# A six-layer transformer on one core: the products, copies and vector steps of a round placed by quarters

## The chip, the cores and the metric

One NeuronCore of a Trainium2 chip runs the whole program in one launch. The metric is device time in microseconds (us), lower is better. The engines are TensorE (PE; its weight loads PEld), VectorE (DVE), ScalarE (ACT), GpSimd (POOL) and SyncE (SP, which issues the DMAs here). Each takes its own list of instructions in a fixed order, and a wait at one of them holds all that stands behind it in that list.

## What is computed

Two adaptive-layer-norm blocks. Block 0 has a test-time-trained layer and then a six-layer local-attention transformer over 4 sequences of 512 tokens, width 128; block 1 has relative attention and a routed expert layer. The change touches the transformer alone:

```python
for i in range(DEPTH):                                   # 6; B 4, n 512, HEADS 16, DIM_HEAD 64
    x = attn_layer(shift_tokens(x), Wqkv[i], q_scale[i], k_scale[i], Wo[i]) + x
    x = ffn_layer(shift_tokens(x), ln_g[i], ln_b[i], W1[i], b1[i], W2[i], b2[i]) + x

def attn_layer(x, Wqkv, qs, ksc, Wo):
    q, k, v = split_heads(x @ Wqkv)
    q, k = l2norm(q) * qs, l2norm(k) * ksc
    q = q * cos * scale + rotate_half(q) * sin * scale   # rotary tables; k with 1 / scale
    k = k * cos * inv + rotate_half(k) * sin * inv
    return merge_heads(local_attention(q, k, v)) @ Wo    # windows of 32, each sees itself and the one before

def ffn_layer(x, g, bln, W1, b1, W2, b2):
    a, gate = split((layernorm(x) * g + bln) @ W1 + b1)
    return a * gelu(gate) @ W2 + b2
```

## The kernel before

**Units, parts, rounds.** A unit is one sequence in one layer: 24 units. Three kinds of work run side by side for different units. (1) Projections of a unit, in 8 pieces (4 of K, 4 of Q); each piece has two halves, one PSUM bank each. (2) Attention of the unit in 8 parts: 4 tiles of 128 tokens, each in two parts, even and odd, by head. (3) The feed-forward of an earlier unit. `rounds()` counts time in steps; a unit starts every `UNIT` steps, a piece and a part every fourth step, a tile of values every eighth. Four steps are called a round here. In each step every engine writes down what its tables `PART_AT`, `NORM_AT`, `SPREAD_AT`, `SCALE_AT`, `FFN_AT` and the lags place there: parts first, then units, the oldest first. That alone sets the order on each engine; the semaphore waits are written beside each instruction and follow the data.

**A piece.** PE: half 0 and half 1, each three fp32r products of weights and input split into high and low (`three_products`, L1111 to L1113). ACT: a square of each half (L1293, `sq`). DVE: four rotary steps out of the two banks (L1421, `kT`, `qT`, `rotated`). POOL: the sum of the two squares (L1556), then two steps that finish the rotation (L1562, L1563). After every second piece PE sums the squares over rows (L1142, 8 products per piece, fp32), DVE takes them into `norms` (L1431), and after each kind come the roots (L217 to L226). K's roots go through DRAM and come back wide (SP, L957), and scale K (DVE, L1444). Q's are turned (PE, L1146) and copied (ACT, L1298).

**A part.** PE: mask and scores (L1203, L1211). DVE: `keep` (L1486), row maxima (L1491). ACT: eight exponentials with sums (L1357). DVE: reciprocal (L1494). POOL: scaling of p (L1577). PE: turn (L1219, four transposes). ACT: copy of p (L1363). PE: weigh (L1229), p times values. ACT: copy of o (L1368). After an odd part PE mixes with Wo (L1237) and DVE adds to z (L1498).

**Values.** For each tile two value products (L1111 to L1113 with `wqkv` as the moving side), each copied by ACT (L1306), then ten window DMAs (SP, L972 to L977).

**Feed-forward.** PE: center, sum, spread (L1162, L1167, L1173), three gate products (L1180), three up products (L1183), down (L1188); the third of each has 85 rows. ACT: gate copies (L1341), gelu (L1345). DVE: `act` times up (L1464), the last addition (L1468).

**PSUM.** Scores have banks 0 and 1, turn 2, weigh 2 and 3, the halves 4 and 5. Sums, value products, mixes, the turned roots and all feed-forward products share banks 6 and 7 in turn (`ring_take`): a product there waits until the last user but one has been read.

Of the kernel before, what the change touches and what calls it, by code (L numbers as in the profile page):

```python
# [11 lines left out]
ALU = mybir.AluOpType  # L12
# [5 lines left out]
B, S = 4, 512  # L18
# [679 lines left out]
def test_time_pool(c, t, later):  # L698
# [4 lines left out]
    for x in range(DOUBLINGS + 1):  # L703
# [5 lines left out]
UNITS_TF, UNIT, TILE, PART = DEPTH * B, 32, 8, 4  # L709
PARTS = 2 * TPB  # L710
GROUPS_TF, HALF_D = 4, DH // 2
PART_FIRST = 39
PART_AT = {"score": 0, "keep": 0, "largest": 1, "exp": 2, "inverse": 3, "scale": 3, "turn": 5, "turn_copy": 6, "weigh": 6, "o_copy": 8, "mix": 9, "add": 9}
PART_STEPS = 10
VALUE_FIRST, WINDOWS_AT = 29, 31
SHIFT_AT = -4
SQUARES_LAG, SUM_LAG, MADE_LAG = 2, 4, 3
NORM_AT = {"root0": 17, "out": 15, "root1": 33, "turn": 39, "copy": 39}
SPREAD_AT = (16, 18, 19, 24)
SCALE_AT = (24, 28, 29, 32)  # L720
HALF_AT = (0, 1)
FFN_AT = {"shift": 80, "center": 83, "square": 84, "sum": 84, "root": 84, "spread": 88, "scale": 89, "gate0": 91, "gate1": 95, "gate2": 96, "gelu": 99,
          "up0": 100, "up1": 101, "up2": 104, "down": 108, "add": 109}
NORM_SPREAD, NORM_SCALE = 2, {1: 9, 2: 17, 3: 25}
NORM_ENDS = (0, B - 1)
TABLES = (2, 3, 0, 1)
UNIT_STEPS = 110
SPLIT_AT = {2: 13, 3: 31, 0: 39, 1: 40, 4: 56, 5: 59}
# [3 lines left out]
def rounds():  # L732

    for r in range(UNIT * (UNITS_TF - 1) + UNIT_STEPS):
        now = [("spread", b, 0) for b in NORM_SCALE if r == NORM_SPREAD] + [("scale", b, 0) for b, at in NORM_SCALE.items() if r == at]
        for m in range(UNITS_TF * PARTS):
            s = r - UNIT * (m // PARTS) - PART_FIRST - PART * (m % PARTS)
            if 0 <= s < PART_STEPS:
                now.append(("part", m, s))
        for u in range(UNITS_TF):  # L740
            s = r - UNIT * u
            if SHIFT_AT <= s < UNIT_STEPS:
                now.append(("unit", u, s))
        yield now
# [98 lines left out]
def ring_takes(kind, n, s):  # L843

    if kind == "part":
        return ["mix"] * (s == PART_AT["mix"] and n % 2)
    users = []
    if kind == "norm":
        return users
    if SUM_LAG <= s < SUM_LAG + UNIT and (s - SUM_LAG) % 8 == 4:  # L850
        users.append(f"sum{(s - SUM_LAG) // 4}")
    if s == NORM_AT["turn"]:
        users.append("rn")
    if 0 <= s - VALUE_FIRST < UNIT and (s - VALUE_FIRST) % TILE in (0, 2):
        i, f = divmod(s - VALUE_FIRST, TILE)
        users.append(f"v{i}{f // 2}")
    users += [name for name in ("center", "sum", "spread", "gate0", "gate1", "gate2", "up0", "up1", "up2", "down") if FFN_AT[name] == s]
    return users
# [59 lines left out]
def transformer_sync(c, t):  # L918
    SP = c.SP
    for now in rounds():  # L920
        for kind, u, s in now:
# [3 lines left out]
            if b == B - 1 and l + 1 < DEPTH:  # L925
                if s == PART_FIRST + PART * (PARTS - 1) + PART_STEPS - 1:
                    SP.wait_ge(*t.mixed.on((u + 1) * TPB - 1))
                    load_mix(c, t, l + 1)
                if s == FFN_AT["add"]:
                    SP.wait_ge(*t.f_down.on(u))  # L930
                    load_ffn(c, t, l + 1)
                for x, k in enumerate(order()):
                    then, after = (l + 1, x + RAW) if x + RAW < len(SPLIT_AT) else (l + 2, x + RAW - len(SPLIT_AT))
                    if s == SPLIT_AT[k] + 1 and then < DEPTH:
# [185 lines left out]
def unit_tensor(c, t, u, s):  # L1120
    PE, psum, (l, b) = c.PE, c.psum, divmod(u, B)
    xs = [x[:, :] for x in t.xs[u % 2]]
    for at in range(2):
        if not (0 <= s < UNIT and s % 4 == HALF_AT[at]):
            continue
        p = s // 4
# [8 lines left out]
    if SUM_LAG <= s < SUM_LAG + UNIT and (s - SUM_LAG) % 8 == 4:  # L1135
        p = (s - SUM_LAG) // 4
# [11 lines left out]
    if 0 <= i < TPB and at in (0, 2):  # L1148
        f = at // 2
# [132 lines left out]
def unit_scalar(c, t, u, s):  # L1282
# [4 lines left out]
    for half in range(2):  # L1287
        p, at = divmod(s - 1 - HALF_AT[half], 4)
# [10 lines left out]
    i, at = divmod(s - VALUE_FIRST - 1, TILE)  # L1299
    if 0 <= i < TPB and at in (0, 2):  # L1300
        n, f = u * TPB + i, at // 2
# [19 lines left out]
def feed_scalar(c, t, u, s):  # L1321
# [14 lines left out]
    for j, (lo, n) in enumerate(CHUNKS):  # L1336
        if s == FFN_AT[f"gate{j}"] + 1:
# [65 lines left out]

def unit_vector(c, t, u, s):
    V, own, psum, (l, b) = c.V, c.v_own, c.psum, divmod(u, B)
    p, at = divmod(s - 2, 4)
    if 0 <= p < 2 * GROUPS_TF and at == 0:
        kind, g, lo = piece(p)
        cos, sin = (t.tab[:, 2 * (1 - kind) + x, :] for x in range(2))
        first, second = (t.scales[:, kind, half, l:l + 1] for half in range(2))  # L1410
        V.wait_ge(*t.squared.on((u, (p, 0))))
        if u or p:
            V.wait_ge(*t.made.on((u, p - 1) if p else (u - 1, 2 * GROUPS_TF - 1)))
        if u >= 2:
            V.wait_ge(*t.scored.on((u - 1) * PARTS - 1))
        first_half, second_half = made_of(t, u, kind, g)
        rot = [first_half, t.turned_by[0][:, :], second_half, t.turned_by[1][:, :]]
        for half, scale, outs in ((0, first, ((0, cos), (3, sin))), (1, second, ((1, sin), (2, cos)))):
            V.wait_ge(*t.squared.on((u, (p, half))))
            for x, table in outs:  # L1420
                last = V.e.scalar_tensor_tensor(out=rot[x], in0=psum[:, 4 + half, :], scalar=scale, in1=table, op0=ALU.mult, op1=ALU.mult)  # L1421
            last.then_inc(*t.rotated.by((u, (p, half))))
    p, at = divmod(s - SUM_LAG - 1, 4)
# [24 lines left out]
def feed_vector(c, t, u, s):  # L1448
# [11 lines left out]
    for j, (lo, n) in enumerate(CHUNKS):  # L1460
        if s == FFN_AT[f"up{j}"] + 1:
# [84 lines left out]
def unit_gpsimd(c, t, u, s):  # L1546
# [3 lines left out]
    p, at = divmod(s - SQUARES_LAG, 4)  # L1550
# [6 lines left out]
    p, at = divmod(s - MADE_LAG, 4)  # L1557
# [938 lines left out]
```

## Time and profile before

| | |
|---|---|
| median of 3 runs | 2498.02 us (2496.93 to 2498.21) |
| the profiled execution | 2506.73 us |
| its span | 2504.8 us |
| busy: PE, DVE, ACT, POOL | 94%, 69%, 64%, 58% |
| mean granted clock of PE | 0.966 of full |

The span runs from the first to the last instruction. The rows below are of this one execution, and times of day in them are us from the start of its span. Matmuls overlap, so that the distance of two starts on PE tells more than an instruction's own length. "Waits" name the instruction that released an engine; "issue" is time in which it waited for nothing that the profile shows.

### The profile page before, as it was taken

How to read it: one execution, taken by the hardware profiler on the slowest of the kernel's cores; microseconds unless marked ns; L12 is line 12 of the kernel's file. 1: busy time of each engine (PE TensorE's matmuls, PEld its weight loads, DVE VectorE, ACT ScalarE, POOL GpSimd, SP SyncE). 2: the span in 40 equal slices, each digit the busy share in tenths (PEclk: the TensorE clock that was granted, in tenths of full speed). 3: DMA queues.
4: the chain of work that ended last, by engine and by line, in shares of the span. 5: the costliest groups of instructions: out<-in, count | busy, mean ns of one | idle time of the engine just before them, and what ended most of it. 6: DMA issues, size and time to landing. Idle time of an engine off the chain costs nothing.

```text
span 2504.8 us, 121652 instructions
## 1 busy us (share of the span) xinstructions
PE 2354.9 (94%) x53677; PEld 1748.5 (70%) x53677; DVE 1717.0 (69%) x3393; ACT 1597.2 (64%) x5036; POOL 1451.3 (58%) x1408
## 2 busy tenths in 40 slices
PE   9958999999999999999999999999888999999967
PEld 8836777777777777677777777777645666666657
DVE  4477788777888888787788788887335555555534
ACT  3226777777777787777777778777625454545422
POOL 1166667656676676566666677665117656656307
PEclk9969999999999999999999999999979999999978
DMA  4013333433333334333343333333216222222136
GB/s 91 15 33 86 79 83 94 97 80 83 91 93 95 82 83 103 83 92 87 80 96 90 80 92 87 87 87 87 54 30 177 49 48 48 48 48 48 31 97 249
DMA packets 230208, 204.60 MB, mean 82 GB/s; under 512 B 133687, under 2 KB 155464, under 8 KB 229552
## 3 DMA queue, kind: packets, MB, share of 16 engines
q1 hardware_dynamic: 225296, 190.91, 30.5%
q8 instruction: 422, 6.91, 1.2%
q0 software_dynamic: 2208, 5.58, 0.7%
q14 instruction: 106, 0.87, 0.1%
q10 hardware_dynamic: 2176, 0.33, 0.1%
HBM read 86.05 MB, written 15.70 MB: 41 GB/s over the span
## 4 chain that ended last, share of the span: by engine, by line
PE 66%; DVE 12%; SPq 6%; ACT 5%; issue 5%; POOL 4%; DMA 3%; POOLq 0%; ACTq 0%; DVEq 0%
PE psum L1211 7%; PE psum L1959 5%; PE psum L1237 5%; PE psum L1229 5%; PE psum L1938 4%; PE psum L1111 4%; PE psum L1944 3%; PE psum L1113 3%; PE psum L1112 3%; PE psum L1993 3%; PE psum L1983 3%; ACT p L1357 3%; SPq L972 3%; PE psum L1188 2%; PE psum L1219 2%
## 5 line engine op out<-in xcount | busy, mean ns | idle before, releaser
L1357 ACT ACTIVATE p<-p,stat 128x64 f32<-128x64 f32 x1536 | 512.4, 336 | 47.2 <-DVE stat L1491 44.9
L1577 POOL TENSOR_TENSOR p<-p,inverse 128x512 f32<-128x512 f32 x192 | 200.2, 1043 | 456.5 <-DVE inverse L1494 452.2
L1211 PE MATMUL psum<-kT,qT 32*32 32x64 f32 x24576 | 305.5, 224 | 25.8 <-issue 24.2
L2092 DVE TENSOR_REDUCE largest<-psum 128x1 f32<-128x512 f32 x256 | 165.0, 687 | 228.0 <-PE psum L1944 228.0
L1211 PEld LDWEIGHTS psum<-kT,qT 32*32 32x32 f32 x24576 | 264.1, 103 | 75.3 <-issue 74.3
L1357 ACT ACTIVATION_READ_ACCUMULATOR p<-p,stat 128x1 f32 x1536 | 288.6, 188 | 0.0
L1421 DVE SCALAR_TENSOR_TENSOR rotated<-psum,scales,rotary 128x512 f32<-128x512 f32 x384 | 270.8, 742 | 25.8 <-ACT sq L1293 25.8
L1556 POOL TENSOR_TENSOR squares<-sq 128x512 f32<-128x512 f32 x192 | 245.3, 1278 | 44.3 <-ACT sq L1293 43.8
L1293 ACT ACTIVATE sq<-psum 128x512 f32<-128x512 f32 x384 | 213.7, 582 | 57.3 <-PE psum L1113 54.6
L1229 PEld LDWEIGHTS psum<-pT,v_win 64*64 64x64 f32 x12288 | 198.6, 136 | 64.7 <-issue 45.9
L1111 PE MATMUL psum<-xs,wqkv_high 128*128 128x512 f32 x384 | 205.7, 536 | 23.2 <-DVE rotated L1421 22.9
L2014 ACT ACTIVATE w_by_key<-psum 128x512 f32<-128x512 f32 x128 | 76.4, 597 | 230.1 <-PE psum L1959 230.1
L1229 PE MATMUL psum<-pT,v_win 64*64 64x32 f32 x12288 | 220.1, 221 | 2.8 <-ACT pT L1363 1.8
L1237 PEld LDWEIGHTS psum<-oT,wo 128*128 128x128 f32 x1536 | 187.9, 196 | 38.5 <-issue 26.3
L1237 PE MATMUL psum<-oT,wo 128*128 128x128 f32 x1536 | 198.2, 283 | 9.0 <-ACT oT L1368 5.6
L1363 ACT ACTIVATE pT<-psum 128x512 f32<-128x512 f32 x192 | 114.2, 595 | 130.4 <-PE psum L1219 130.3
L1306 ACT ACTIVATE v_tok<-psum 128x512 f32<-128x512 f32 x192 | 113.8, 593 | 101.8 <-PE psum L1113 73.9
L1444 DVE TENSOR_TENSOR kT<-kT,rnorm_wide 128x1024 f32<-128x1024 f32 x96 | 164.0, 1728 | 13.4 <-DMA rnorm_wide<-rnorms 13.3
L2104 POOL TENSOR_TENSOR q_by_head<-q_heads,mask_head 64x256 fp32r<-64x256 f32 x252 | 157.5, 625 | 15.4
L2060 ACT ACTIVATE weights<-psum,largest 128x512 f32<-128x512 f32 x256 | 161.5, 687 | 3.7 <-DVE largest L2092 3.7
L1421 DVE SCALAR_TENSOR_TENSOR kT<-psum,scales,rotary 128x512 f32<-128x512 f32 x192 | 142.3, 741 | 28.2 <-ACT sq L1293 14.4
L1563 POOL TENSOR_TENSOR qT<-qT,rotated 128x512 f32<-128x512 f32 x96 | 157.9, 1645 | 0.0
(351 smaller groups left out, 5402.3 us busy)
## 6 DMA issues: line engine op xcount, KB each, us to landing
v_win<-v_tok SPq DMA_DIRECT2D x576, 128.0 KB
rnorm_wide<-rnorms SPq DMA_DIRECT2D x384, 64.0 KB
v_win<-v_tok SPq DMA_DIRECT2D x336, 64.0 KB
q_rows<-q_rows_all SPq DMA_DIRECT2D x32, 512.0 KB, 4.6
tile_weights<-expert_table SPq DMA_DIRECT2D x23, 512.0 KB, 5.8
wqkv<-L_ffn_Wqkv SPq DMA_DIRECT2D x96, 64.0 KB, 2.2
rel_values<-sq SPq DMA_DIRECT2D x60, 64.0 KB, 2.2
wo<-L_ffn_Wo SPq DMA_DIRECT2D x48, 64.0 KB
```

What stands on the lines that cost most here:

```text
L1111: PE.e.matmul(out, w[0], x[1], start=True, stop=False)
L1211: last = PE.e.matmul(psum[WIN * blk:WIN * (blk + 1), f, out], q[rows, g, half, tok:tok + WIN], k[rows, g, half, tok:tok + 2 * WIN], start= ...
L1229: last = PE.e.matmul(psum[to:to + DH, 2 + o, at:at + WIN], v[rows, blk, 2 * (2 * a + o) + h, :], t.pt[h][rows, 2 * a + o, blk * WIN:(blk + ...
L1237: last = PE.e.matmul(ps[:, 0:P], t.wo[:, e, :], t.ot[e % 2][:, e // 2, :], start=(e == 0), stop=(e == PAIRS - 1))
L1293: A.e.activation(t.sq[half][:, :], c.psum[:, 4 + half, :], ACT.Square).then_inc(*t.squared.by((u, (p, half))))
L1357: last = A.e.activation(p, p, ACT.Exp, bias=t.stat[:, h, 2 * g + f:2 * g + f + 1], accum_out=t.sum[:, h, g, f:f + 1])
L1421: last = V.e.scalar_tensor_tensor(out=rot[x], in0=psum[:, 4 + half, :], scalar=scale, in1=table, op0=ALU.mult, op1=ALU.mult)
L1444: V.e.tensor_tensor(k, k, t.wide[g % 2][:, :].unsqueeze(1).to_broadcast([P, 2, S]), ALU.mult).then_inc(*t.k_scaled.by((u, g)))
L1556: G.e.tensor_tensor(t.sq_both[p % 2][:, :], t.sq[0][:, :], t.sq[1][:, :], ALU.add).then_inc(*t.squares.by((u, p)))
L1577: G.e.tensor_tensor(p, p, t.inv[:, h, :, :].unsqueeze(3).to_broadcast([P, GROUPS_TF, 2, 2 * WIN]), ALU.mult).then_inc(*t.p_scaled.by(m))
L2060: A.e.activation(t.e[n % 4][:, :], c.psum[:, n % 5, :], ACT.Exp, bias=t.mx[n % 4][:, 0:1]).then_inc(*t.exped.by(n))
L2092: V.e.tensor_reduce(t.mx[n % 4][:, :], psum[:, n % 5, :], AX, ALU.max, negate=True).then_inc(*t.largest.by(n))
```

## The change

The count of steps is made four times as fine: a round has 16 steps instead of 4, and all tables are written in these quarters. Most entries are the old ones times four. These are not:

- PE: the sum of squares now stands at the first step of a round and half 0 at the next (`HALF_AT` (1, 4), sum at 0); before, both had the same step and half 0 was written first. Up product 0 goes to the step of up product 1 (404), behind weigh; before it stood behind turn.
- ACT: squares at 4 and 8, copy of o at 6 between them, value copies at 11 of the round and at 2 of the next, so behind the second square.
- DVE: row maxima two steps behind `keep`, ahead of the addition (L1498) that stood ahead of them; both `act` times up steps (0 and 1) at 404, ahead of the reciprocal. The four rotary steps are written by a new function `rotate`, in the same order.
- ACT, once a layer: one copy of weights (L1317, `wqkv_high`) goes ahead of the next copy of p.

```diff
-PART_AT = {"score": 0, "keep": 0, "largest": 1, "exp": 2, "inverse": 3, "scale": 3, "turn": 5, "turn_copy": 6, "weigh": 6, "o_copy": 8, "mix": 9, "add": 9}
+PART_AT = {"score": 0, "keep": 0, "largest": 2, "exp": 8, "inverse": 12, "scale": 12, "turn": 20, "turn_copy": 24, "weigh": 24,
+           "o_copy": 26, "mix": 36, "add": 36}
...
-HALF_AT = (0, 1)
+HALF_AT, SQUARE_AT, ROTATE_AT = (1, 4), (4, 8), (8, 8)
...
     for at in range(2):
-        if not (0 <= s < UNIT and s % 4 == HALF_AT[at]):
+        p, late = divmod(s - HALF_AT[at], PIECE)
+        if late or not 0 <= p < 2 * GROUPS_TF:
             continue
...
     for half in range(2):
-        p, at = divmod(s - 1 - HALF_AT[half], 4)
+        p, at = divmod(s - SQUARE_AT[half], PIECE)
...
-    i, at = divmod(s - VALUE_FIRST - 1, TILE)
-    if 0 <= i < TPB and at in (0, 2):
-        n, f = u * TPB + i, at // 2
+    i, at = divmod(s - VALUE_FIRST, TILE)
+    for i, at in ((i, at), (i - 1, at + TILE)):
+        if not (0 <= i < TPB and at in VALUE_COPY_AT):
+            continue
+        n, f = u * TPB + i, VALUE_COPY_AT.index(at)
...
     for j, (lo, n) in enumerate(CHUNKS):
-        if s == FFN_AT[f"up{j}"] + 1:
+        if s == FFN_AT[f"gated{j}"]:
```

The orders of SP and POOL are the same row by row, and so is the order in which the shared PSUM banks are taken. Instructions, shapes and waits are the same on every engine. The lines of the changed kernel stand 4 to 12 further down.

**PE, the round with up products 0 and 1** (L1237 mix, L1219 turn, L1183 up, L1229 weigh). Before:

```order
L1237 MATMUL psum<-oT,wo 128x128 x8
L1219 MATMUL psum<-ident,p 128x128 x4
L1183 MATMUL psum<-sq,w 128x512
L1111 MATMUL psum<-xs_1,wqkv_high 128x512
L1112 MATMUL psum<-xs_0,wqkv_low 128x512
L1113 MATMUL psum<-xs_0,wqkv_high 128x512
L1229 MATMUL psum<-pT,v_win 64x32 x32
L1183 MATMUL psum<-sq,w 128x512
L1111 MATMUL psum<-wqkv_low,xs_0 128x512
L1112 MATMUL psum<-wqkv_high,xs_1 128x512
L1113 MATMUL psum<-wqkv_high,xs_0 128x512
```
Now:

```order
L1241 MATMUL psum<-oT,wo 128x128 x8
L1223 MATMUL psum<-ident,p 128x128 x4
L1115 MATMUL psum<-xs_1,wqkv_high 128x512
L1116 MATMUL psum<-xs_0,wqkv_low 128x512
L1117 MATMUL psum<-xs_0,wqkv_high 128x512
L1233 MATMUL psum<-pT,v_win 64x32 x32
L1187 MATMUL psum<-sq,w 128x512 x2
L1115 MATMUL psum<-wqkv_low,xs_0 128x512
L1116 MATMUL psum<-wqkv_high,xs_1 128x512
L1117 MATMUL psum<-wqkv_high,xs_0 128x512
```
The first up product left its place behind turn; both stand behind weigh, ahead of the value product.

**PE, the round with up product 2** (L1142, now L1146, is the sum of squares). Before:

```order
L1219 MATMUL psum<-ident,p 128x128 x4
L1183 MATMUL psum<-sq,w 85x512
L1111 MATMUL psum<-xs_1,wqkv_high 128x512
L1112 MATMUL psum<-xs_0,wqkv_low 128x512
L1113 MATMUL psum<-xs_0,wqkv_high 128x512
L1142 MATMUL psum<-squares,onehot 32x128 x8
L1229 MATMUL psum<-pT,v_win 64x32 x32
```
Now:

```order
L1223 MATMUL psum<-ident,p 128x128 x4
L1187 MATMUL psum<-sq,w 85x512
L1146 MATMUL psum<-squares,onehot 32x128 x8
L1115 MATMUL psum<-xs_1,wqkv_high 128x512
L1116 MATMUL psum<-xs_0,wqkv_low 128x512
L1117 MATMUL psum<-xs_0,wqkv_high 128x512
L1233 MATMUL psum<-pT,v_win 64x32 x32
```
The sum stands ahead of half 0 and behind the feed-forward product, in place of between half 0 and weigh.

**ACT, a round with a value copy** (L1357 exponentials, L1293 squares, L1306 value copy, L1368 copy of o). Before:

```order
L1363 ACTIVATE pT<-psum 128x512
L1357 ACTIVATE p,sum<-p,stat 128x64 x8
L1293 ACTIVATE sq<-psum 128x512
L1306 ACTIVATE v_tok<-psum 128x512
L1293 ACTIVATE sq<-psum 128x512
L1368 ACTIVATE oT<-psum 128x2x2x128
```
Now:

```order
L1369 ACTIVATE pT<-psum 128x512
L1363 ACTIVATE p,sum<-p,stat 128x64 x8
L1297 ACTIVATE sq<-psum 128x512
L1374 ACTIVATE oT<-psum 128x2x2x128
L1297 ACTIVATE sq<-psum 128x512
L1312 ACTIVATE v_tok<-psum 128x512
```
The copy of o moved from the end to between the squares, the value copy from between them to the end.

## Rows read from the trace of the kernel before

**Rows 1.** The page: busy time of each engine; the chain that ended last, by engine.
```profile
PE 2354.9 (94%) x53677; PEld 1748.5 (70%) x53677; DVE 1717.0 (69%) x3393; ACT 1597.2 (64%) x5036; POOL 1451.3 (58%) x1408
...
PE 66%; DVE 12%; SPq 6%; ACT 5%; issue 5%; POOL 4%; DMA 3%; POOLq 0%; ACTq 0%; DVEq 0%
```

**Rows 2.** Stretches: start:end, length, busy time (x instructions) of each engine, clock, DMA.
```profile
528.00:596.00 68.00, 67.21 (x1827) 50.33 (x1825) 56.02 (x110) 53.44 (x185) 44.11 (x35) 1.00 0.34 88
```

**Rows 3.** Waits of 188 to 1752: engine, its line <- awaited: total us, times, longest.
```profile
PE psum L1211 <- issue: 22.2, 40, 1.3
...
PE psum L1111 <- ACT v_tok L1306: 6.2, 6, 2.8
...
PE psum L1219 <- POOL p L1577: 4.4, 9, 1.0
...
PE psum L1237 <- ACT oT L1368: 4.3, 10, 1.1
...
ACT v_tok L1306 <- DMA v_win<-v_tok: 24.7, 16, 4.1
```

**Rows 4.** Timeline of PE: start us, length us, operation, [idle before <-awaited]; first units.
```profile
209.43 3.47 PE L1237 MATMUL psum<-oT,wo 128*128 128x128 f32 x16 [1.05 <-ACT oT L1368]
...
236.98 0.97 PE L1219 MATMUL psum<-ident,p 128*128 128x128 f32 x4 [2.74 <-ACT oT L1368]
```

**Rows 5.** Timeline of PE, a round with a bare turn before half 0.
```profile
475.47 0.60 PE L1219 MATMUL psum<-ident,p 128*128 128x128 f32 x4
475.83 0.48 PE L1111 MATMUL psum<-xs,wqkv_high 128*128 128x512 f32 x1
...
477.28 1.14 PE L1229 MATMUL psum<-pT,v_win 64*64 64x32 f32 x64
```

**Rows 6.** Timeline of PE, the round with gate product 2, sum first.
```profile
511.03 0.60 PE L1219 MATMUL psum<-ident,p 128*128 128x128 f32 x4
511.46 1.02 PE L1180 MATMUL psum<-sq,w 128*85 128x512 f32 x2
512.41 0.65 PE L1142 MATMUL psum<-squares,onehot 128*32 128x128 f32 x16
512.99 0.50 PE L1111 MATMUL psum<-xs,wqkv_high 128*128 128x512 f32 x1
513.33 0.39 PE L1112 MATMUL psum<-xs,wqkv_low 128*128 128x512 f32 x1
...
513.89 1.14 PE L1229 MATMUL psum<-pT,v_win 64*64 64x32 f32 x64
```

**Rows 7.** Timeline of PE, the round with up product 2, half 0 first.
```profile
528.07 1.02 PE L1183 MATMUL psum<-sq,w 128*85 128x512 f32 x2
...
530.29 1.14 PE L1229 MATMUL psum<-pT,v_win 64*64 64x32 f32 x64
```

**Rows 8.** Timeline of PE, the round with up products 0 and 1.
```profile
519.51 0.60 PE L1219 MATMUL psum<-ident,p 128*128 128x128 f32 x4
...
521.61 1.14 PE L1229 MATMUL psum<-pT,v_win 64*64 64x32 f32 x64
522.67 1.12 PE L1183 MATMUL psum<-sq,w 128*128 128x512 f32 x2
523.23 0.80 PE L1111 MATMUL psum<-wqkv_low,xs 128*128 128x512 f32 x1
523.87 0.40 PE L1112 MATMUL psum<-wqkv_high,xs 128*128 128x512 f32 x1
```

**Rows 9.** Timeline of DVE, the step behind up product 0.
```profile
522.07 0.74 DVE L1464 SCALAR_TENSOR_TENSOR act<-psum,b1c,act 128x512 f32<-128x512 f32 x1
```

**Rows 10.** Timeline of ACT, the copy of o in the round of L1146.
```profile
526.28 0.59 ACT L1368 ACTIVATE oT<-psum 128x512 f32<-128x512 f32 x1
```

**Rows 11.** Timeline of PE, a mix right behind scores.
```profile
804.99 2.05 PE L1237 MATMUL psum<-oT,wo 128*128 128x128 f32 x16 [0.19 <-ACT oT L1368]
```

**Rows 12.** Timeline of PE, the value product behind L1146.
```profile
526.85 0.48 PE L1111 MATMUL psum<-wqkv_low,xs 128*128 128x512 f32 x1
```

More of the change, by code:

```diff
@@ L735, in rounds @@
         now = [("spread", b, 0) for b in NORM_SCALE if r == NORM_SPREAD] + [("scale", b, 0) for b, at in NORM_SCALE.items() if r == at]
-        for m in range(UNITS_TF * PARTS):
-            s = r - UNIT * (m // PARTS) - PART_FIRST - PART * (m % PARTS)
+        for m in range(max(0, (r - PART_FIRST - PART_STEPS) // PART), min(UNITS_TF * PARTS, (r - PART_FIRST) // PART + 1)):
+            s = r - PART_FIRST - PART * m
             if 0 <= s < PART_STEPS:
                 now.append(("part", m, s))
-        for u in range(UNITS_TF):
+        for u in range(max(0, (r - UNIT_STEPS) // UNIT), min(UNITS_TF, (r - SHIFT_AT) // UNIT + 1)):
             s = r - UNIT * u
@@ L933, in transformer_sync @@
                     then, after = (l + 1, x + RAW) if x + RAW < len(SPLIT_AT) else (l + 2, x + RAW - len(SPLIT_AT))
-                    if s == SPLIT_AT[k] + 1 and then < DEPTH:
+                    if s == SPLIT_AT[k] + LOAD_LAG and then < DEPTH:
                         SP.wait_ge(*t.split_low.on((l + 1, k)))
@@ L1147, in unit_tensor @@
     i, at = divmod(s - VALUE_FIRST, TILE)
-    if 0 <= i < TPB and at in (0, 2):
-        f = at // 2
+    if 0 <= i < TPB and at in VALUE_AT:
+        f = VALUE_AT.index(at)
         PE.wait_ge(*split_on(t, l, 4))
@@ L1336, in feed_scalar @@
     for j, (lo, n) in enumerate(CHUNKS):
-        if s == FFN_AT[f"gate{j}"] + 1:
+        if s == FFN_AT[f"gate_copy{j}"]:
             A.wait_ge(*t.f_gates.on((u, j)))
@@ L1401, in transformer_vector, with rotate @@
                 unit_vector(c, t, n, s)
+def rotate(c, t, u, p, half):
+    V, psum, (l, b), (kind, g, lo) = c.V, c.psum, divmod(u, B), piece(p)
+    cos, sin = (t.tab[:, 2 * (1 - kind) + x, :] for x in range(2))
+    V.wait_ge(*t.squared.on((u, (p, half))))
+    if u or p:
+        V.wait_ge(*t.made.on((u, p - 1) if p else (u - 1, 2 * GROUPS_TF - 1)))
+    if u >= 2:
+        V.wait_ge(*t.scored.on((u - 1) * PARTS - 1))
+    first, second = made_of(t, u, kind, g)
+    if half == 0:
+        outs = ((first, cos), (t.turned_by[1][:, :], sin))
+    else:
+        outs = ((t.turned_by[0][:, :], sin), (second, cos))
+    for out, table in outs:
+        last = V.e.scalar_tensor_tensor(out=out, in0=psum[:, 4 + half, :], scalar=t.scales[:, kind, half, l:l + 1], in1=table, op0=ALU.mult, op1=ALU.mult)
+    last.then_inc(*t.rotated.by((u, (p, half))))
 def unit_vector(c, t, u, s):
     V, own, psum, (l, b) = c.V, c.v_own, c.psum, divmod(u, B)
[L1406 to L1423, printed above, removed]
+    for half in range(2):
+        p, at = divmod(s - ROTATE_AT[half], PIECE)
+        if 0 <= p < 2 * GROUPS_TF and at == 0:
+            rotate(c, t, u, p, half)
+    p, at = divmod(s - COUNT_LAG, PIECE)
     if 0 <= p < 2 * GROUPS_TF and at == 0 and p % 2:
```

55 lines of the change are left out of this document (28 added, 27 removed).

## The prediction

> **What bounds the kernel now.** I read the page first: TensorE (PE) is busy 94% of the span, and in the chain that ended last PE has 66% while no other engine passes 12% [rows 1]. Then the stretches. The layers' attention fills the time from 188 to 1753 us; a unit follows the last some 68 us later, and in a settled stretch of that length PE is busy 67.2 of 68 us at full clock, VectorE (DVE) 56.0, ScalarE (ACT) 53.4, GpSimd (POOL) 44.1 [rows 2]. So in the layers a round lasts as long as PE's own list. Last, the waits from 188 to 1752 us [rows 3]. PE waited 22.2 us for "issue" (nothing that the profile shows), and the change leaves the number of PE instructions alone. Waits that an order can touch are small: 6.2 us for the copy of values, 4.4 for the scaled p, 4.3 for the copy of o and 2.7 more in one place [rows 4]: 17.6 us, 0.7% of the whole. Two questions follow: which of these 17.6 us go, and what the new order of PE costs PE itself.
>
> **The change part by part.** A term is per round or unit, in the steady part. "Plain" means the distance of two starts when nothing is waited for.
>
> *1. The sum of squares (L1142) moves ahead of the first projection half, on PE.* Before, PE runs turn (L1219), half 0 (L1111 to L1113), sum, weigh (L1229): from 475.47 to 477.28, 1.81 us [rows 5]. The new order exists once per unit already, in the round of gate 2. From it I take the pieces: turn to the next fp32 product 0.43, sum to half 0 to weigh 513.89 - 512.41 = 1.48 [rows 6]. 0.43 + 1.48 = 1.91, so +0.10 us. With a feed-forward product of 85 rows between turn and the rest both orders stand in the trace: half 0 first 530.29 - 528.07 = 2.22 [rows 7], sum first 513.89 - 511.46 = 2.43 [rows 6], so +0.20 us. The printed order moves 68 sums: 25 behind a bare turn, 22 behind the spread product (priced as bare), 21 behind the 85-row product. 47 x 0.10 + 21 x 0.20 = **+8.9 us**. PE is the bound, nothing lies over it. The reason that I see: fp32 products drain before an fp32r projection starts usefully (L1111 to L1112 takes 0.64 behind L1183 and 0.34 behind the sum [rows 6, 8]), and the old order shared that drain.
> What does the sum wait for, 0.8 us earlier? For GpSimd's squares and for its PSUM bank, whose last user but one is a value product with its copy. Both are ready before the new place in every settled unit. Twice in the first units the squares end some 0.3 us behind it; I book 0.6 there. Bounds of the term: 0 (orders equally good) to 68 x 0.21 = 14.
>
> *The Trainium skill on this.* The page "TensorE: Matmul & The Clock Gate", section "Part 2: What happens when you issue a matmul", says that weight loads are pulled ahead of running products while the products keep their order, so the next tile's weights load beside this tile's work. By that the swap is free and the sum would be 8.9 us smaller. The two orders [rows 6, 7] speak against it; it is the second rival below.
>
> *2. Up products 0 and 1 both stand behind weigh, and their two DVE steps (L1464) go together.* Before, up 0 ran behind turn, and the value product (whose bank it frees) started usefully at 523.87 - 0.34 = 523.53, 4.02 us behind turn at 519.51 [rows 8]. Now: turn to half 0 0.36 [rows 5] and on to weigh 0.88, together 1.24; weigh to up 0 1.06; up 0's end 1.12 later [rows 8]; DVE step 0.74 [rows 9]; hand-overs some 0.1. That is 4.26, and weigh is now met by the end of the copy of p (turn's 0.60 and the copy's 0.60), some 0.05 more: 4.3. So PE waits for DVE here where it did not: +0.3 us. Behind that wait on PE stand the value product, half 1 and the next scores; up 1 runs ahead of it and covers the rest. 22 units: **+6.6 us**. Bounds: 0 (DVE answers within up 1) to 0.6 a unit, 13. The second step now runs ahead of the reciprocal; both wait for less than the exponentials, which end later, so this costs nothing. PE's own work is equal: a block of this kind adds 0.56 and 0.30 (0.64 - 0.34) to what follows, 0.86, at either place.
>
> *3. The copy of o (L1368) goes between the two squares of ACT.* It ends some 0.5 us earlier in rounds without a value copy (a square of the same size goes behind it; such an operation takes 0.59 [rows 10] and the next starts 0.1 before its end). Mixes that stand right behind scores gain: 14 of them start at the end of this copy, as at 804.99 with a wait of 0.19 [rows 11], each 0.13 to 0.42 us late against the others, 2.5 us in all. Five of these lie in the round whose turn then waits for p (4.4 us in all [rows 3]), behind the DVE chain of roots that the change does not shorten; there the gain is taken back. I take **-1.5 us**. The second square comes up to 0.5 us later: DVE is then still on the first half's two steps, so nothing.
>
> *4. The start of the layers.* Units 0 and 1 have no feed-forward, so rounds are short and the copy of o is late: PE waits 1.05 us at 209.43 and 2.74 at 236.98 (behind a value copy that waits for a DMA) [rows 4]. The first loses 0.5, the second some 1.3 of it, two more 0.5 each: -2.8. The value product after the first L1146 loses 1.0, since its bank's copy now comes last on ACT. With the 0.6 of part 1: **-1.2 us**. The mix at 209.43 took 3.47 us where 2.05 is plain [rows 4, 11]: the clock granted fell to its lower level (1.2 GHz) behind that wait. If a fall goes, 1.4 us more do; I take one: **-1.4**.
>
> *5. Value copies behind the squares.* Bank by bank, the only PE product that meets this is the one behind L1146. The copy that frees its bank now ends where o's did, 526.28 + 0.59 = 526.87, against a start of 526.85 [rows 10, 12]. Alone that costs 0 to 0.2 us a unit. But part 2 makes PE 0.3 later just ahead of it while ACT's chain starts at turn: it is covered, 0. If part 2 costs nothing, this costs 0.2 x 22 = 4 instead.
>
> *6. Row maxima ahead of the addition (DVE).* The maxima come up to 0.3 us earlier, but the exponentials stand behind the copy of p on ACT, which waits for turn: 0. The addition, 0.7 later, frees the bank of up 1, which is needed later still: 0. The first half's sum feeds the roots 0.8 us earlier; their DMA stands in SyncE's queue behind ten window DMAs, so nothing starts earlier. The orders of SyncE and GpSimd are the same row by row. One weight copy a layer goes ahead of p's copy on ACT, 5 times some 0.6 us, in rounds whose turn does not wait for p: 0, at most 3.
>
> Sum: 8.9 + 6.6 - 1.5 - 1.2 - 1.4 = +11.4, less some 0.6 where PE's late value waits (6.2 us, bound to DMAs [rows 3]) swallow part of a delay: **+11 us**. The profiled execution took 2506.73 us (span 2504.8), so 2518 there; against the median, 2498.02, that is **2509 us**, 0.44% slower. What a measurement here can tell from no change is 0.2%, 5 us.
>
> **The rivals.**
> (a) *PE's order is free*: the next operand is in place whichever product runs, the 8.9 us fall away, and part 2 stays. 11 - 8.9 = +2: 2500 us. The rule of the Trainium skill above would have it so. For it: the distances 2.43 and 2.22 are of different feed-forward products (gate and up). Against: same shapes, and the bare turn gives a cost too. No change.
> (b) *Faster: the copy of o carries it.* If the waits of [rows 3] are one coupled delay, and an earlier o takes all 17.6 us and two falls of the clock (2.8), while PE's order costs its 8.9 and DVE answers up 0 in time: -17.6 - 2.8 + 8.9 = -11.5, some 2487 us. It decides once the waits removed pass those 8.9 us (15.5 if part 2 costs too). For it: PE waits on o at every point of the first units. Against: the largest is a DMA's, the second the roots', and neither moves.
> (c) *More waits come*: the value product behind L1146 is not covered, and late copies meet the gate-1 round, where the value product already waits 6.2 us: 0.2 to 0.3 us a unit on top, +5: 2514 us.
> (d) *It does nothing* beyond noise because the rounds are bound elsewhere: [rows 2] leave 0.8 of 68 us for that; I put it in with (a).
>
> **How the numbers follow.** Forecast 0.48 (its own range 2503 to 2514), (a) and (d) 0.24, (b) 0.16, (c) 0.12. The range leaves out most of (b) and the top of (c): 2493 to 2516. Slower by over 0.2% (over 2503): forecast and (c), 0.60; within: 0.24; faster: 0.16.
>
> **What would show it.** Right: some 0.5 us more per unit between two L1146 (68 us now) with no more "issue"; turn to weigh 1.9 us in the round now 1.81; a new PE wait for L1464's successor (act, DVE) once per unit of 0.2 to 0.3 us; mix right behind scores at plain distance; the L1219 waits for p unchanged. Wrong: turn, sum, half 0, weigh in 1.8 us or less (then a), no wait for act, or waits for p and values gone (then b).

## The result, and the profile after

Six runs of the changed kernel have a median of 2513.09 us (2509.53 to 2516.08), six of the kernel before on the same chip 2495.66 us (2491.94 to 2498.21): ratio 1.0070, 95% interval 1.0055 to 1.0084, so **17.4 us slower**, 0.70%. The forecast was slower by 11 us, so the loss is 6 us larger than forecast. The median itself lies only 4 us above the forecast's 2509 and still in the likeliest case's own range (2503 to 2514), because six runs put the kernel before 2.4 us lower than the 2498.02 that the forecast started from: some luck. A second comparison gave 1.0069 (1.0045 to 1.0094).

The first pair of profiled executions tells much less than that: spans of 2507.6 and 2504.8 us. One execution carries several us of chance, and the first one of the kernel before carried much of it, as a second trace of each kernel shows below. So times are compared by medians here, and a trace is read for distances that repeat.

The lines of the changed kernel are numbered 4 to 12 higher: sum L1146, halves L1115 to L1117, turn L1223, weigh L1233, mix L1241, up products L1187 and their DVE step L1476, copy of o L1374. Its page: busy times, the chain that ended last, and ACT's exponentials.

```profile
span 2507.6 us, 121657 instructions
...
PE 2368.5 (94%) x53677; PEld 1746.3 (70%) x53677; DVE 1734.7 (69%) x3393; ACT 1594.9 (64%) x5036; POOL 1460.0 (58%) x1408
...
PE 78%; POOL 5%; DVE 5%; issue 4%; ACT 3%; SPq 2%; DMA 2%; POOLq 0%; ACTq 0%; DVEq 0%
...
L1363 ACT ACTIVATE p<-p,stat 128x64 f32<-128x64 f32 x1536 | 512.0, 336 | 20.1 <-DVE stat L1503 17.3
```

PE executes the same 53677 products and is busy 13.6 us longer than in [rows 1]; its share of the last chain rises from 66% to 78%. ACT waits 17.3 us for the row maxima where it waited 44.9 before. All of that moved, and none of it is time, as PE was the bound and still is.

PE's waits in the changed kernel from 188 to 1752 us (engine, line <- awaited: total us, times, longest), and then those of its weight loads (PEld), which the profile keeps apart:

```profile
PE psum L1215 <- issue: 18.6, 39, 1.2
PE psum L1223 <- POOL p L1589: 4.9, 9, 0.9
PE psum L1115 <- ACT v_tok L1312: 2.7, 6, 1.2
PE psum L1241 <- issue: 2.7, 3, 1.2
PE psum L1146 <- POOL squares L1568: 2.0, 3, 0.9
```

```profile
PEld psum L1115 <- DVE act L1476: 18.5, 21, 0.9
```

Against [rows 3]: the waits for the copy of o (4.3 us) are gone, those for the value copy fell from 6.2 to 2.7, those for the scaled p stayed (4.4 and 4.9), "issue" did not grow, and the squares of GpSimd are new with 2.0. PE's listed waits thus fell, while the kernel became slower. The new wait for `act` is there, 21 times, but on the row of the weight loads and not of the products: a product whose weights wait starts when the previous one's modelled end is just past, so the profile shows PE as busy.

**Where the time comes from.** For all rounds from 255 to 1745 us I took the distances turn to weigh and weigh to turn, kind by kind, less the waits that PE's rows show. Two traces of each kernel agree on these medians to 0.01 us, except the last line's (us):

```
distance on PE                                   before       changed      rounds
turn, (sum, half 0 in either order), weigh       1.80         2.00         22
the same with the spread product behind turn     2.69-2.70    2.90         22
the same with the 85-row up product              2.66         2.86         21
turn, (up 0 before only), half 0, weigh          2.14         1.34         21
weigh, (up 0 now), up 1, ... to the next turn    6.03-6.04    7.20         21
weigh, ..., mix, turn (rounds without others)    5.73-5.77    5.65-5.71    43
```

Lines 1 to 3 are the sum of squares: +0.20 us x 65 = **+13.0 us**. Lines 4 and 5 are the pair of up products: 1.34 + 7.20 - 2.14 - 6.03 = +0.37, and turn to turn of the same rounds 8.16 before and 8.55 now, +0.39, x 21 = **+8 us**. That makes 21; the 4 us down to 17 are what is left over, not a measurement. The sixth line bears 0.02 to 0.12 us x 43 of them, 1 to 5 us. Most of that lies in the rounds with the third up product: behind weigh they are 0.14 us shorter in both traces (5.61 against 5.76 and 5.75), x 21 = 3 us.

The bare round at the same place as [rows 5], in the changed kernel (timeline of PE: start, length, operation):

```profile
475.25 0.60 PE L1223 MATMUL psum<-ident,p 128*128 128x128 f32 x4
475.78 0.65 PE L1146 MATMUL psum<-squares,onehot 128*32 128x128 f32 x16
476.35 0.51 PE L1115 MATMUL psum<-xs,wqkv_high 128*128 128x512 f32 x1
...
477.25 0.55 PE L1233 MATMUL psum<-pT,v_win 64*64 64x32 f32 x24
```

Start to start: 0.53 + 0.57 + 0.90 = 2.00. Before it was 0.36 + 0.87 + 0.58 = 1.81 [rows 5; the sum's start there is 476.70]. Turn to sum alone takes 0.53, where turn to a product of tile 128*128 takes 0.36 (projection, fp32r) or 0.44 (fp32; it is the same ahead of the spread and down products, and 0.43 to 0.44 ahead of the 85-row ones):

```profile
484.23 0.60 PE L1223 MATMUL psum<-ident,p 128*128 128x128 f32 x4
484.67 0.95 PE L1171 MATMUL psum<-ones,sq 128*128 128x1 f32 x8
```

The round with the up products, against [rows 8]: PE, its weight loads, and DVE.

```profile
518.81 1.14 PE L1233 MATMUL psum<-pT,v_win 64*64 64x32 f32 x64
519.88 1.98 PE L1187 MATMUL psum<-sq,w 128*128 128x512 f32 x4
521.92 0.50 PE L1115 MATMUL psum<-wqkv_low,xs 128*128 128x512 f32 x1
```

```profile
518.81 1.02 PEld L1233 LDWEIGHTS psum<-pT,v_win 64*64 64x64 f32 x64 [0.43 <-ACT pT L1369]
...
520.84 0.19 PEld L1187 LDWEIGHTS psum<-sq,w 128*128 128x128 f32 x1 [0.22 <-issue]
521.91 0.19 PEld L1115 LDWEIGHTS psum<-wqkv_low,xs 128*128 128x128 f32 x1 [0.88 <-DVE act L1476]
```

```profile
521.11 1.54 DVE L1476 SCALAR_TENSOR_TENSOR act<-psum,b1c,act 128x512 f32<-128x512 f32 x2 [0.72 <-PE psum L1187]
```

Weigh waits for ACT's copy of p (the 1.34 in place of 1.29). DVE stands idle until up 0 has ended (521.11), its two steps take 0.77 each, so the first ends at 521.88, and the value product's weights load at 521.91, 4.45 us behind turn (517.46).

### The profile page after: what moved, and what is told of

It is laid out like the page before. It is cut to its first block, busy times and chain, and to the rows that moved or that the text cites. A ratio compares the mean times of both kernels' runs of the same rounds, so it can differ in the third digit from the quotient of the medians.

```text
span 2507.6 us, 121657 instructions
## 1 busy us (share of the span) xinstructions
PE 2368.5 (94%) x53677; PEld 1746.3 (70%) x53677; DVE 1734.7 (69%) x3393; ACT 1594.9 (64%) x5036; POOL 1460.0 (58%) x1408
## 4 chain that ended last, share of the span: by engine, by line
PE 78%; POOL 5%; DVE 5%; issue 4%; ACT 3%; SPq 2%; DMA 2%; POOLq 0%; ACTq 0%; DVEq 0%
PE psum L1215 9%; PE psum L1233 7%; PE psum L1115 6%; PE psum L1241 6%; PE psum L1971 5%; PE psum L1950 4%; PE psum L1117 4%; PE psum L1116 4%; PE psum L1956 3%; PE psum L2005 3%; PE psum L1223 3%; PE psum L1995 3%; PE psum L1192 3%; PE psum L1184 2%; PE psum L1146 2%
## 5 line engine op out<-in xcount | busy, mean ns | idle before, releaser
L1363 ACT ACTIVATE p<-p,stat 128x64 f32<-128x64 f32 x1536 | 512.0, 336 | 20.1 <-DVE stat L1503 17.3
L1297 ACT ACTIVATE sq<-psum 128x512 f32<-128x512 f32 x384 | 223.9, 583 | 74.5 <-PE psum L1117 72.8
L1233 PEld LDWEIGHTS psum<-pT,v_win 64*64 64x64 f32 x12288 | 197.9, 135 | 76.9 <-issue 49.2
L1233 PE MATMUL psum<-pT,v_win 64*64 64x32 f32 x12288 | 219.1, 221 | 3.1 <-ACT pT L1369 3.1
L1115 PE MATMUL psum<-xs,wqkv_high 128*128 128x512 f32 x384 | 193.4, 504 | 17.4 <-DVE rotated L1425 17.0
L1241 PEld LDWEIGHTS psum<-oT,wo 128*128 128x128 f32 x1536 | 187.5, 196 | 31.6 <-issue 25.9
L1241 PE MATMUL psum<-oT,wo 128*128 128x128 f32 x1536 | 197.7, 283 | 3.6 <-issue 2.7
L1425 DVE SCALAR_TENSOR_TENSOR kT<-psum,scales,rotary 128x512 f32<-128x512 f32 x192 | 142.1, 740 | 31.5 <-ACT sq L1297 24.7
L1117 PE MATMUL psum<-xs,wqkv_high 128*128 128x512 f32 x384 | 155.7, 405 | 0.0
L1116 PE MATMUL psum<-xs,wqkv_low 128*128 128x512 f32 x384 | 155.0, 404 | 0.0
```

What stands on the lines that cost most here:

```text
L1115: PE.e.matmul(out, w[0], x[1], start=True, stop=False)
L1116: PE.e.matmul(out, w[1], x[0], start=False, stop=False)
L1117: return PE.e.matmul(out, w[0], x[0], start=False, stop=True)
L1233: last = PE.e.matmul(psum[to:to + DH, 2 + o, at:at + WIN], v[rows, blk, 2 * (2 * a + o) + h, :], t.pt[h][rows, 2 * a + o, blk * WIN:(blk + ...
L1241: last = PE.e.matmul(ps[:, 0:P], t.wo[:, e, :], t.ot[e % 2][:, e // 2, :], start=(e == 0), stop=(e == PAIRS - 1))
L1297: A.e.activation(t.sq[half][:, :], c.psum[:, 4 + half, :], ACT.Square).then_inc(*t.squared.by((u, (p, half))))
```

## The experiments

Each was timed in five rounds beside the kernel before on the same chip. The medians there are about 2506 to 2510 us for the kernel before, so ratios count; "us" below is ratio x 2500. An interval is 3 to 6 us wide on either side, and a difference of two kernels is less sure than that, 5 to 7 us.

```
kernel          ratio to before (95%)       us against before
change_again    1.0069 (1.0045 to 1.0094)   +17
pe_as_before    0.9983 (0.9970 to 0.9997)   -4
pe_as_before_2  0.9988 (0.9972 to 1.0005)   -3
sum_as_before   1.0016 (0.9997 to 1.0034)   +4
up_as_before    1.0023 (1.0009 to 1.0037)   +6
act_as_before   1.0062 (1.0039 to 1.0084)   +16
value_late      1.0034 (1.0014 to 1.0054)   +9
maxima_alone    0.9993 (0.9976 to 1.0010)   -2
o_alone         1.0009 (0.9989 to 1.0028)   +2
o_and_maxima    0.9992 (0.9977 to 1.0007)   -2
before_again    0.9999 (0.9981 to 1.0017)   0
sum_late        1.0665 (1.0641 to 1.0689)   +166
```

**Both moves on PE undone** (against the changed kernel):

```
-HALF_AT, SQUARE_AT, ROTATE_AT = (1, 4), (4, 8), (8, 8)
+HALF_AT, SQUARE_AT, ROTATE_AT = (0, 4), (4, 8), (8, 8)
-"up0": 404   "gated1": 404
+"up0": 400   "gated1": 408
```

> The changed kernel with both moves on TensorE undone: the sum of squares runs behind projection half 0 again, and up product 0 runs behind turn, its DVE step a quarter-round earlier than that of up product 1. The earlier copy of o, the value copies behind the second square, the earlier row maxima and the weight copy stay as changed. My theory (the moves on PE are what costs, priced now from the trace of the changed kernel at 0.20 us x 65 rounds = 13 for the sum and 0.34 x 21 = 7 for the up pair): the time falls by some 20 us from 2513, to about 2493, thus 0 to 4 us below the kernel before, the small rest being what the copy of o gives. Rival 'the order on PE is free and the loss is in ACT's and DVE's new order': it stays near 2513. Rival 'the copy of o carries a large gain that the moves on PE hide': below 2488.

Measured 0.9983: 21.7 us less than the changed kernel, more than its whole loss of 17.4, and so faster than the kernel before. The interval leaves out 1; the repeat's (0.9988) does not.

> pe_as_before once more, beside the three others: whether its ratio of 0.9983 to the kernel before holds. Expected 0.997 to 1.000.

The rivals "the order on PE is free" and "a large gain is hidden" both fall. A few us are left for everything else that the change does.

**The sum alone undone** (`HALF_AT` back to (0, 4)):

> The changed kernel with one thing undone: the sum of squares runs behind projection half 0 again (68 places). My theory: the distance turn to weigh goes from 2.00 back to 1.80 us in the bare round and by the same 0.20 in the two kinds of rounds with a feed-forward product, so 13 us less than the changed kernel, about 2500 us (the term on record was 8.9, which would give 2504). Rival 'order is free': 2513, and the distances stay at 2.00.

Measured 1.0016, 13 us less than the changed kernel, some 6 either way. The bare round is back at 1.80 us, the two others at 2.70 and 2.66:

```profile
475.32 0.60 PE L1223 MATMUL psum<-ident,p 128*128 128x128 f32 x4
475.68 0.48 PE L1115 MATMUL psum<-xs,wqkv_high 128*128 128x512 f32 x1
...
476.56 0.64 PE L1146 MATMUL psum<-squares,onehot 128*32 128x128 f32 x16
477.13 1.14 PE L1233 MATMUL psum<-pT,v_win 64*64 64x32 f32 x64
```

**The up pair alone undone** (`up0` 400, `gated1` 408):

> The changed kernel with one thing undone: up product 0 runs behind turn and its DVE step a quarter-round ahead of that of up product 1; the sum of squares stays ahead of half 0. My theory: the wait of the value product's weight load for the DVE step (22 times in the changed kernel) goes, 0.34 us x 21 = 7 us less, about 2506 us (the term on record: 6.6). Rival (PE's own work grew when two of these products stand together, no wait): also 7 us less, but the value product would stand the same distance behind the DVE step's end as before. Rival 'free': 2513. If the sum, now ahead of half 0, meets the up product behind turn, the term is smaller.

Measured 1.0023: 11.7 us less than the changed kernel, with an uncertainty of some 5, so 8 fits, and so would 10. The trace has 8.32 us turn to turn in these rounds in place of 8.55, 0.23 less by the medians (0.29 by the means, 21 rounds): with up 0 back, the value copy behind the second square, covered until then, costs some 0.1 of its own (below). So rows bear 5 to 6 us here; the rest of the 11.7 is in no distance that I found, and within the uncertainty.

**The value product behind half 1**, both up products still together (`VALUE_AT` from (0, 8) to (1, 8)):

> The changed kernel with the first value product of each pair behind projection half 1 instead of ahead of it, on TensorE only; both up products still stand together behind weigh. My theory (the value product waits for DVE to finish the step of up product 0): half 1 takes over those 0.3 us, so weigh to turn in the round of the up products goes from 7.20 to about 6.9 us, the 22 waits of its weight load for DVE go, and the kernel is 6 to 7 us faster than the changed one. Rival (two such products in a row simply take PE longer): 7.20 stays, no gain. What could spoil both: the value product comes 0.7 us later in all 96 of its rounds, and its copy on ACT with it.

Measured 1.0034, 9 us less, some 6 either way. Weigh to turn is 6.89 (7.20), turn to turn 8.18 (8.55 in the changed kernel, 8.16 before), the wait is gone, and half 1 follows up 1 by itself:

```profile
519.72 1.98 PE L1187 MATMUL psum<-sq,w 128*128 128x512 f32 x4
521.14 0.79 PE L1115 MATMUL psum<-xs,wqkv_high 128*128 128x512 f32 x1
```

```profile
521.11 0.19 PEld L1115 LDWEIGHTS psum<-xs,wqkv_high 128*128 128x128 f32 x1 [0.24 <-issue]
```

The next product now starts 1.42 us behind the pair's start (2.04 in the changed kernel; its first product then takes 0.63 to the next in place of 0.33, so 0.3 net). The same four instructions of the two up products stand in a row as in the changed kernel, and 0.02 us is left of the pair's cost, so their neighbourhood costs next to nothing; the wait for DVE was the rest. PE's order cannot be called costly or free as such: this pair is free, the sum is not.

**ACT's copies undone** (`o_copy` 26 to 32, `VALUE_COPY_AT` (7, 14) to (4, 12)):

> The changed kernel with the order of ACT's copies undone: the copy of o runs last of its round again and the value copies stand before the second square and before the copy of p as they did. PE, DVE, GpSimd and SyncE keep the changed order. On record: the copy of o gives 1.5 us in the steady part and some 1 to 2 in the first units, so 1 to 4 us slower than the changed kernel, 2514 to 2517. Rival 'the copy of o carries a large gain': 2523 or more, since waits for o and for values then come back in full (17 us of them stood in the kernel before, 3 in the changed one). Rival 'the value copies behind the squares cost': faster than 2513.

Measured 1.0062, 2 us faster than the changed kernel and within the uncertainty the same. The waits did come back in its trace, 6.0 us for o and 3.2 for values, and ACT's own wait for window DMAs with them:

```profile
PE psum L1223 <- ACT oT L1374: 4.2, 3, 2.8
...
PE psum L1241 <- ACT oT L1374: 1.8, 3, 0.7
```

```profile
ACT v_tok L1312 <- DMA v_win<-v_tok: 20.3, 15, 3.5
```

In the changed kernel that last row reads 8.8 us in 13 waits, in the kernel before 24.7 [rows 3]. The changed kernel's own traces have 2.7 and 2.0 us of waits for o and values, so some 7 us more of such rows came with no more time (2 us less, some 7 either way). The rival "large gain" falls, "value copies cost" gets no support, and a gain of 1 to 4 us can be neither shown nor excluded here.

**Parts alone, on the kernel before.** Row maxima and weight copy:

> The kernel before with two small parts of the change alone: row maxima a half round-part earlier on DVE (ahead of the addition), and one weight copy a layer ahead of the copy of p on ACT. TensorE's order and all other copies as before. My forecast books 0 for both: within 0.2% of the kernel before (5 us). Rival (the earlier exponentials are what gains, since ACT waited 44.9 us for the row maxima before and 17.3 after the change): 4 us or more faster.

0.9993: no change that can be told, as booked, though ACT's wait for the maxima fell from 44.9 and 42.8 (two traces of before) to 38.7 us. In the round with the third up product, turn to turn falls from 8.42 and 8.41 us (before) to 8.36. The copy of o:

> The kernel before with one part of the change alone: on ScalarE the copy of o goes from last place of its round to between the two squares; value copies, row maxima and all of TensorE stay as before. On record: 1.5 us in the steady part and 1 to 2 in the first units, so 1 to 4 us faster than the kernel before. Rival 'it carries a large gain': 10 us or more faster. If it is not resolved (the interval of such a comparison is 3 to 4 us wide on either side), the trace decides: rounds with a mix should be shorter by some 0.1 us, and PE's waits for the copy of o (7.0 and 3.1 us in the two traces of the kernel before) should be near 0.

1.0009, not resolved, with the larger part of its interval on the slower side. The trace has PE's waits for o down to 1.1 us, as said, but its waits for p up at 7.2 (4.4 and 5.4 before), and rounds with a mix no shorter: a mean of 6.11 us with waits, 6.13 and 6.04 before. The round with the third up product stays at 8.41. Both together:

> The kernel before with the earlier copy of o, the earlier row maxima and the earlier weight copy, and nothing else of the change: pe_as_before with the value copies put back as well. In pe_as_before the stretch weigh to turn of the L1150 round takes 6.16 us where the kernel before takes 6.03, which I put down to the value product that waits for the value copy now behind the squares. My theory: 6.03 comes back, so some 2 to 3 us faster than pe_as_before, about 0.9975 of the kernel before. Rival (the 0.1 us is not the value copy's): 6.16 stays, the time equals pe_as_before.

0.9992 (pe_as_before 0.9983 and 0.9988): the times do not resolve 2 us. The distance does. Weigh to turn in the L1150 round (L1146 before) has a mean of 6.04 us here, 6.13 and 6.12 in the two traces of pe_as_before and 6.03 in both of the kernel before, so 0.09 us x 22 = 2 us (0.13 and 3 us by the medians) belong to the value copies behind the second square. And the round with the third up product takes 8.27 here, 8.28 and 8.27 in pe_as_before and 8.27 in sum_as_before: 0.14 us less than before, x 21 = 3 us. Its stretch from scores to mix is what shrinks, from 1.68 to 1.53 us. With the early o alone nothing of it shows, with the early maxima and weight copy alone less than half of it (8.36), and act_as_before, which has these but o late, has it too (8.47, as the changed kernel has with its sum moved). So the small gain that stands beside PE's order comes with the maxima and the weight copy rather than with o. Why they need a second move beside them no run shows.

**The kernel before, once more.**

> The kernel before, unchanged, once more: the width of the measurement itself, and a second trace of it. Both theories: ratio 1.000 with an interval that holds 1. In the trace: turn to weigh 1.80 us in the bare round with a sum, no wait of a value product behind up 0; the part from the first turn to the last near 1619 us or a few us shorter, because the first trace had one 2.8 us wait of PE behind a late window DMA.

> The changed kernel, unchanged, once more, beside the kernel before and the other kernels of this call. My theory: 1.006 to 1.008 of the kernel before (some 17 us), as in its first comparison. If the order on PE were not the cause and only chance in its first comparison, the ratio would be nearer 1.001, as the spans of the first two profiled executions (2507.6 and 2504.8) would have it.

Null comparison 0.9999. Spans 2502.9 and 2521.2, so this pair differs by 18.3 us where the first pair differed by 2.8. First turn to last turn takes 1619.3 and 1605.9 us in the two traces of the kernel before and 1620.1 and 1624.5 in those of the changed one. The first trace of before had 6.2 us of waits for values and 7.0 for o, the second:

```profile
PE psum L1237 <- ACT oT L1368: 2.3, 4, 0.7
...
PE psum L1219 <- ACT oT L1368: 0.8, 1, 0.8
...
PE psum L1111 <- ACT v_tok L1306: 0.5, 2, 0.2
```

That is 9.6 of the 13.4 us. The two traces are of different comparisons, so the chance of one execution and a difference between the comparisons are not told apart. Of the 17.6 us that the prediction called "waits that an order can touch" the second trace has 9.0: half of them were of that one execution.

**The sum at a third place** (pe_as_before with `SUM_LAG` 20, `COUNT_LAG` 24 and both roots 4 later):

> pe_as_before with the sum of squares moved to yet another place on TensorE: behind projection half 1, with DVE's step on it and the roots a quarter-round later. My theory (the sum costs more only right behind turn, because a sum behind turn starts 0.53 us after it where a projection starts 0.36 after it; behind a projection its price is 0.57 to 0.58 us): nothing changes against pe_as_before, within 3 us, turn to weigh is 1.29 us in every bare round, and the round's rest is longer by some 0.5 us. Rival (its price depends on the weigh product that follows it): weigh to turn grows by 0.7 or more, 13 us slower than pe_as_before.

A miss: 6.7% slower. The local distances show one thing of use: what each place of the sum costs PE itself. From turn to the mask product, waits left out (medians, us; tile changes counted up to there):

```
round               order behind turn                          us           tile changes
bare                half 0, sum, weigh, half 1 (before)        3.67-3.68    3
bare                sum, half 0, weigh, half 1 (changed)       3.87-3.88    4
bare                half 0, weigh, half 1, sum (sum_late)      3.88         4
up product 2        half 0, sum, weigh, half 1 (before)        4.54         3
up product 2        sum, half 0, weigh, half 1 (changed)       4.73         4
up product 2        half 0, weigh, half 1, sum (sum_late)      4.62         4
gate product 2      sum, half 0, weigh, half 1 (both)          4.73         4
gate product 2      half 0, weigh, sum, half 1 (sum_late)      4.54         3
```

My expectation had the sum dear only right behind turn, and this is wrong: behind half 1 it costs the bare round as much (0.08 of it in a weigh that starts 0.98 behind half 0 in place of 0.90). The last row is an order that neither kernel has: the sum between weigh and half 1, 0.19 us shorter, since sum_late moved it there in this one kind of round. What I had not priced is the step that reads the sum. It runs a quarter-round later on DVE, behind the rotations, and it is what frees the PSUM bank that the next mix takes:

```profile
PE psum L1115 <- DVE z L1510: 36.2, 20, 1.8
PE psum L1115 <- DVE rotated L1425: 28.0, 19, 3.3
PE psum L1241 <- DVE norms L1443: 20.7, 26, 1.7
PE psum L1187 <- DVE z L1510: 14.9, 19, 0.8
```

The mix waits for the count (L1443), the addition L1510 behind the mix is late, the value and up products wait for that addition, and ACT waits 168.8 us for row maxima. The users of the two banks come in the same order in both kernels, so only DVE's place moved against PE's. These rows sum to 100 us of the 166; the rest I did not trace.

## Why the prediction was right, and where it was off

*What bounds the kernel*: right. PE's list sets the round. ACT's and DVE's waits changed by tens of us without effect, and the changes of PE's own distances add up to those of the time, within the 5 to 7 us that a difference of two kernels is unsure.

*1. The sum ahead of half 0*: the mechanism was right, the size was off, booked 8.9, measured 13.0 by the distances and 13 by the time (sum_as_before). The step that failed is "turn to the next fp32 product 0.43": I took the start of a gate product for that of the sum. The sum starts 0.53 behind a bare turn, and behind the spread product, which I "priced as bare", it costs 0.20 too. The price for the 85-row round, taken from two whole rounds that stood in the trace, was exact (0.20). The bound of 14 held. The cause that I named (the old order "shared that drain" of fp32 products) is not what the bare round shows: there half 0's first product takes 0.32 to its second behind turn (before) and 0.35 behind the sum (changed), not 0.64. What the rows do show has two parts. One is the type: behind turn an fp32 product of the same tile starts after 0.44, half 0 after 0.36, and the new order puts the fp32 sum there, +0.08. The other is the tile: turn and half 0 use 128*128, the sum 128*32, weigh 64*64. Where the tile changes, the next start is late by 0.07 to 0.10: turn to sum 0.53 where turn to an fp32 product of tile 128*128 is 0.44, half 0 to sum 0.87 and to weigh 0.90 where three products of a value or half are 0.80 ahead of the next (521.92 to 522.72 in the changed kernel). 0.08 + 0.09 + 0.10 - 0.07 is the 0.20. The old order changes tile three times from turn to half 1, the new one four times. The Trainium skill has this rule on the page "TensorEngine Tiling (Array Packing)", section "Key Properties": changing the tiling mode, not just the tile, drains TensorE. The rows agree; it gives no time, and by the rows here a change is worth some 0.1 us. The orders of sum_late fit in sign: one change more and 0.08 to 0.20 longer, one change fewer and 0.19 shorter. That the tile changes are the larger part of the cause is read from these orders and not isolated by a run.

*Rival (a), order is free*: refuted in the distances and in the time, since pe_as_before is 21.7 us faster than the changed kernel. The rule on weight loads that the prediction took from the Trainium skill ("TensorE: Matmul & The Clock Gate", "Part 2: What happens when you issue a matmul") is not contradicted as such, but what I concluded from it, a free swap, is: the load of the sum starts with its product (475.78 both), 0.53 behind turn.

*2. Up products together*: the mechanism was right; booked 6.6 with a wait of 0.3 us, measured 0.39 x 21 = 8, and value_late removes it (0.37 by the distance; 9 us by the time, some 6 either way). My working had the value product 4.3 us behind turn; it stands 4.45 behind. Half 0 to weigh is 0.90 to 0.93, not 0.88, and DVE starts 1.23 behind up 0 (519.88 to 521.11), not 1.12; the 0.05 for weigh being late was there in 13 or 14 of the 21 rounds.

*3. The copy of o* (-1.5) and *4. the first units* (-1.2, -1.4): the sum does not resolve. All that is left beside PE's order gives -4 and -3 us in two comparisons, near the -4.1 booked for these terms, but 3 us of it lie in the round with the third up product and do not come with the copy of o (o_alone), so that the agreement is in part luck. The first turn to the twelfth takes 90.0 and 89.7 us in the changed kernel, 91.6 and 91.2 before: -1.5 us, with the sum's extra there included. The fall of the clock is less clear: a mix of 3.3 to 3.6 us (2.05 plain) stands at 209.43 in the first trace of before (granted clock 0.60 from 209 to 213) and at 244.83 in the second, in neither of the changed kernel, but in traces of seven other kernels somewhere from 211 to 247, sum_as_before, up_as_before and value_late among them, which have the early copy of o. Whether the change removes it stays open. I had booked 0.6 for the sum's wait for GpSimd's squares; it took 2.0 and 0.9.

*5. Value copies behind the squares*: "alone that costs 0 to 0.2 us a unit" is 0.09, and in the changed kernel it is covered by part 2, as said: pe_as_before has it, and the changed kernel's 7.20 has DVE's wait ahead of it. What I missed is a gain beside it: behind the second square ACT meets the window DMAs later, 8.8 and 8.7 us of waits in the two traces of the changed kernel against 24.7 and 15.9. I had written that the DMA's wait does not move. It does, though PE hardly sees it. The early copy of o may have a part in it: o_alone, whose value copies are where they were, has 12.0.

*6. Maxima and weight copy*: booked 0, and the time agrees (0.9993, 0.9976 to 1.0010), but the distances have the 3 us above with them.

*The other rivals*: (b) had its waits right (o's went, v's mostly) and its price wrong, half of it being of one execution. (c), more waits, did not come; its number, 2514, is nearest to the median for another reason: my first term was 4 us too small and the second 1.

*What would show it*: right on 0.5 us more per unit (the 60 turns from the 32nd on: 67.96 and 67.55 us a unit before, 68.11 and 68.65 changed, a mean of +0.6; over all 160 from there +0.45, and by the first pair of traces alone only +0.1), on "issue" and on turn's waits for p. Wrong in the row: the wait for act is on the weight loads, and the bare round takes 2.00, not 1.90.

## What to carry to other kernels

Price a swap on a bound TensorE by whole rounds of both orders that already stand in the trace, not by pieces from other neighbours; count the changes of tile in each order as well as the products. When a product's PSUM bank is freed by another engine's step, look at the weight loads' row of the waits, since PE's own row can call that time busy. And before a wait of one execution is booked as a gain, take it from a second trace: with a few us at stake, one span of 2.5 ms says little.

## What the runs showed of the hardware

- A wait can be invisible on PE and stand on its weight loads: 18.5 us in 21 waits (0.9 each), of which 0.3 to 0.4 each were time (value_late).
- With the same products in another order PE needs 0.20 us more for turn, sum, half 0 and weigh, by the medians of all three kinds of rounds. Of the bare round's 0.20, 0.08 goes with the type of the product behind turn and 0.12 with the tile changes, as read from neighbouring rows.
- The sum between weigh and half 1 costs no more than between half 0 and weigh: turn to mask 4.54 us in rounds with an 85-row product, 4.73 with the sum ahead of half 0.
- Two traces of one kernel differ by 13.4 us over the layers (1619.3 and 1605.9), while the times of its runs against itself gave 0.9999 (0.9981 to 1.0017).
- The part behind the last turn took 691 and 692 us in the first pair of traces and 702 and 701 in the second, whichever the kernel: times of different comparisons are compared by their ratios only.
